# Reading a comparison's node numbers from PSUM, and a GpSimd wait for landed rows at every block's end

## The chip, the core and the metric

The kernel runs on one core of a Trainium2 chip. The metric is the device time of one execution in microseconds (us). Three runs of the kernel before took 4235.66, 4248.94 and 4250.05 us; the median is 4248.94 us. Beside them stands one execution that the hardware profiler recorded, and all durations below are read from it.

The engines are named as the profile names them: PE is TensorE (PEld its weight loads), DVE is VectorE, ACT is ScalarE, POOL is GpSimd, SP is SyncE. A "q" behind a name (POOLq) is the engine's sequencer, which handles waits and branches and hands instructions to the engine.

## The reference

Two layers of a relational graph convolution over 12,500 nodes with 128 channels and 200,000 edges, then a residual and a layer norm. An edge has a type (the argmax over 10 columns of its attributes), a source and a target. For each target node and each type the source rows are averaged, each mean is multiplied by that type's weight matrix, and the ten products are added to a root term and a bias.

```
edge_type = argmax(msg[:, 16:-16], axis=1)            # 10 types
def _rgcn_layer(x, src, dst, edge_type, w_rel, root, bias):
    seg = dst * NUM_REL + edge_type
    sums = segment_sum(x[src], seg, N * NUM_REL)
    cnt = segment_sum(ones, seg, N * NUM_REL)
    mean = (sums / maximum(cnt, 1)[:, None]).reshape(N, NUM_REL, -1)
    return einsum('nrd,rdo->no', mean, w_rel) + x @ root + bias
h = relu(_rgcn_layer(x, ...w_rel1, root1, b1))
out = layernorm(x + _rgcn_layer(h, ...w_rel2, root2, b2))
```

The edges come sorted by target. The kernel has a fast path that relies on this, and a general path behind a flag; with these inputs the fast path runs.

## The kernel before

**Tiling.** The edges are cut into 1563 tiles of 128. Eight tiles are an oct (the last oct has three), two octs belong to a block of 128 target nodes, so a layer has 196 octs and 98 blocks. Seven blocks (PER) are a lap, and 14 laps are a layer. The first and the last lap are written out, the laps between them are a hardware loop on every engine (`laps`, L1259). The two layers run one after the other: layer 2 gathers from the rows that layer 1 wrote.

**POOL (L1288).** For each tile one indirect DMA (`gather`, L1304, its call in the profile as L1305) fetches 128 rows of 512 bytes from memory into `rows[slot, j]`, with the 128 row numbers read from an SBUF tile: `idx_t` for the first 56 gathers, `idx_s` for all others. There are seven slots of eight tiles; oct o uses slot o modulo 7. Every landed gather adds 16 to `rows_in[slot]`. Before an oct, POOL waits for `idx_ready` (L1327), by which ACT says that it has put the oct's numbers into `idx_s`. ACT does this (L1466) as soon as PE has finished the oct that had the slot seven octs earlier. POOL waits for nothing else inside a layer; before layer 2 it waits for `h_saved` (L1323).

**DVE.** For each oct it makes S (`make_S`, L1815): for 8 tiles x 140 columns the comparison of the column numbers 0 to 139 (`iota_c`) with a number per edge (`comb_t`: 10 x the node's place in a window of 14, plus the type). In layer 1 it also makes `hit` and `hit_typ` (L1809, L1811), with which PE counts the edges. Then it adds what PE left in PSUM to a ring of partial sums in SBUF (L1863, and in layer 1 L1836 for the counts), finds the types of edges three blocks ahead (L1781 to L1794), and sums ten products for the block three back (L1899).

**PE.** In `aggregate` (L1585) it waits for S and for the oct's rows (L1588), then multiplies rows by S into one of four PSUM banks. In `transform` (L1611) it multiplies the ring's finished block by the weights. In layer 1 it also turns the types of a block two ahead into `ps_misc` (`turn_types`, L1560), a PSUM bank of 512 columns of which the types take the first 16; DVE copies them out in `take_types` (L1802, L1803).

**Who sets the order.** Each engine's program is written out by hand and runs in order; semaphores tie them. `rows_there` (L1271) gives the count that `rows_in[slot]` has when an oct has landed; before the change only PE uses it.

Of the kernel before, what the change touches and what calls it, by code (L numbers as in the profile page):

```python
# [19 lines left out]
GT = 8  # L20
# [1057 lines left out]
PER = 7  # L1078
# [6 lines left out]
TCOL = TWIN * R  # L1085
# [18 lines left out]
def gnn_kernel(nc, x, src, dst, edge_attr, w_rel1, root1, b1, w_rel2, root2, b2, out, table1, table2,  # L1104
# [5 lines left out]
    with ctx:  # L1110
# [3 lines left out]
        def ps(name):  # L1114
            return ctx.enter_context(nc.psum_tensor(name, [P, 512], F32))
# [19 lines left out]
        held = sem("held")  # L1135
# [14 lines left out]
        S_ready = sem("S_ready")  # L1150
# [101 lines left out]
        ps_agg = [ps(f"ps_agg{q}") for q in range(4)]  # L1252
        ps_y = [ps(f"ps_y{k}") for k in range(3)]
        ps_misc = ps("ps_misc")
        tp_bank = [*ps_y, ps_misc]

        htab = table2[0:N, :]
# [22 lines left out]
        def bc1(ap, n, w):  # L1280
            return ap.rearrange("p (u w) -> p u w", u=1).to_broadcast([P, n, w])
# [6 lines left out]
        @blk.gpsimd  # L1288
        def _(pool):
            g_ = nc.gpsimd  # L1290
            g_.memset(ident[:], 0.0).then_inc(consts_done, 1)
            pool.wait_ge(consts_done, 1)
            g_.affine_select(out=ident[:], in_=ident[:], compare_op=ALU.not_equal, fill=1.0, base=0,
                             pattern=[[-1, P]], channel_multiplier=1).then_inc(consts_done, 1)
            for tile, step, base, mult in ((iota_c, 1, 0, 0), (rev_r, -1, R, 0), (p16, -16, 0, 1), (step_row, P, 0, 0)):
                g_.iota(tile[:], pattern=[[step, tile.shape[1]]], base=base, channel_multiplier=mult,
                        allow_small_or_imprecise_dtypes=True).then_inc(consts_done, 1)
            g_.iota(lap_row[:].rearrange("a (l q) -> a l q", l=LAPS), pattern=[[RN, LAPS], [0, 4 * PER]], base=0,
                    channel_multiplier=0, allow_small_or_imprecise_dtypes=True).then_inc(consts_done, 1)
            g_.memset(eps[:], EPS).then_inc(consts_done, 1)  # L1300
            g_.memset(zero_b[:], 0.0).then_inc(consts_done, 1)
            g_.memset(hit_typ[:], 0.0).then_inc(consts_done, 1)

            def gather(l, slot, j, at):  # L1304
                pool.indirect_dma_start(  # L1305
                    out=rows[:, slot, j, :], out_offset=None, in_=(x, htab)[l][:, :],
                    in_offset=bass.IndirectOffsetOnAxis(ap=at, axis=0)).then_inc(rows_in[slot], 16)


            pool.wait_ge(idx_done, 1)  # L1310
            for o in range(PER):
                for j in range(GT):
                    gather(0, o, j, idx_t[:, o * GT + j:o * GT + j + 1])

            pool.wait_ge(flags_done, 1)
            fast = pool.value_load(flag_i[0:1, 0:1], min_val=0, max_val=1)
            with pool.If(fast < 1):
                pool.wait_ge(clean, 1)
                general_pool(pool)
            with pool.If(fast > 0):  # L1320
                for l in range(2):
                    if l:
                        pool.wait_ge(h_saved, 16 * NBLOCK)  # L1323
                    for i, first, last in laps(pool):
                        for o in range(PER if first and l == 0 else 0, 2 * PER):

                            pool.wait_ge(idx_ready, i * (2 * PER) + (l * OCTS + o + 1 - PER))  # L1327
                            if not isinstance(i, int):
                                pool.sem_inc(held, 1)  # L1329
                            for j in range(tiles_of(o, last)):  # L1330
                                gather(l, o % PER, j, idx_s[:, o % PER, j:j + 1])

        @blk.sync
        def _(sp):
# [202 lines left out]
        def _(pe):  # L1537
# [21 lines left out]
            with pe.If(fast > 0):  # L1559
                def turn_types(s):  # L1560

                    pe.wait_ge(typ_ready, s + 1)
                    for h in range(2):
                        ins = t_.matmul(ps_misc[:, h * GT:(h + 1) * GT], lhsT=typ_a[:, h, :], rhs=pick[:, :],
                                        start=True, stop=True)
                    ins.then_inc(typ_turned, 1)
# [62 lines left out]
                for l in range(2):  # L1629
                    if l == 0:  # L1630
                        turn_types(0)
                        pe.wait_ge(typ_taken, 1)
                        turn_types(1)
                    else:
                        pe.wait_ge(rc_done, NBLOCK)
                        pe.wait_ge(y_taken, NBLOCK * 3 + 3)
                    turn_x(0, l * (LAPS * 16) + 16).then_inc(xt_ready, 1)
                    pe.wait_ge(weights_in[l], 32)
                    for i, first, last in laps(pe):
                        for k in range(PER):  # L1640
                            s = i * PER + k
                            behind = not (first and k < 2)
                            if l == 0 and not (last and k >= PER - 2):
                                pe.wait_ge(typ_taken, s + 2)
                                turn_types(s + 2)
                            if k == 2 and not first:
                                pe.wait_ge(fold_done, i + l * (LAPS - 1))
                            off = offsets(i * (2 * PER) + 2 * k)
                            aggregate(l, i, 2 * k, off, last, ((k - 2) % PER, s * 4 - 2) if behind else None)
                            if behind:  # L1650
                                transform(l, s - 2, (k - 2) % PER, s * 4 - 2,
                                          (i if k > 0 else i - 1) * 16 + (l * LAPS * 16 + 16))
                            off = offsets(i * (2 * PER) + 2 * k + 1)
                            aggregate(l, i, 2 * k + 1, off, last)
                    for b in (NBLOCK - 2, NBLOCK - 1):
                        if l == 0:
                            pe.wait_ge(agg_taken, QUADS + 4)
                            if b == NBLOCK - 1:
                                pe.wait_ge(rc_done, b)
                            turn_counts(ps_misc, 300, b % PER).then_inc(rc_turned, 1)  # L1660
                        transform(l, b, b % PER, QUADS, (l + 1) * LAPS * 16 if b < NBLOCK - 1 else None)

        @blk.vector
        def _(dve):
# [91 lines left out]
            for c in range(1, 4):  # L1756
# [3 lines left out]
            link(v_.tensor_scalar(spread[:, :, :], bc(iota_c[:, 0:16], 16, GT), pm[:, 0:1], -1.0, ALU.is_equal,  # L1760
                                  ALU.mult))

            fast = dve.value_load(flag_i[0:1, 0:1], min_val=0, max_val=1)
            with dve.If(fast < 1):

# [5 lines left out]
            with dve.If(fast > 0):  # L1771
# [41 lines left out]
                                     ).then_inc(hit_ready, 1)  # L1813

                def make_S(g, sl):  # L1815
                    v_.tensor_tensor(S[:, sl, :, :], bc1(iota_c[:, :], GT, TCOL),  # L1816
                                     bc(comb_t[:, bass.ds(g * GT, GT)], GT, TCOL), ALU.is_equal).then_inc(S_ready, 1)

                def places(g):
# [185 lines left out]
```

## Time and profile before

| what | value |
|---|---|
| median of three runs | 4248.94 us |
| profiled execution, own time | 4252.87 us |
| its span | 4251.2 us |
| POOL busy | 3229.2 us, 76% of the span |
| DVE busy | 2271.6 us, 53% |
| PE busy | 2114.3 us, 50% |
| ACT busy | 961.9 us, 23% |
| 16 DMA engines, share of the gathers' queue | 18.4% |
| gathers | 3126 (1507 + 56 in layer 1, 1563 in layer 2) |

A row of the page's fifth part groups the instructions of one line: busy time, the mean of one in ns, and the idle time of the engine just before them with what ended it. "issue" stands for idle time in which the engine waited for nothing that the profile shows. The chain of waits is followed back from the last instruction of the span, or of a window, to whatever released each step. In the chain, a piece "DMA rows<-..." runs from the start of a gather's instruction on POOL to the moment at which its rows have landed.

### The profile page before, as it was taken

Reading aid. Unit: us, or ns where it says so; the run is one execution under the profiler, and the core shown is the slowest. Engines: PE = TensorE matmul, PEld = TensorE weight load, DVE = VectorE, ACT = ScalarE, POOL = GpSimd, SP = SyncE. Lnnn points to the kernel's source line nnn. Section 1 sums busy time; section 2 is a strip of 40 time slices with the busy share of each in tenths; the row PEclk is TensorE's granted clock in tenths of the full one; section 3 lists DMA queues with packets and bytes.
Section 4 is the critical chain, followed back from the end, with each engine's and each line's share of the span. In section 5 each row is a group of like instructions: output and inputs, shape, how many; then the busy total and the mean of one; then the engine's idle time right before and its main releaser. Section 6 shows DMA issues by size and latency. Waiting matters only on the chain.

```text
span 4251.2 us, 55995 instructions
## 1 busy us (share of the span) xinstructions
PE 2114.3 (50%) x12375; PEld 1993.4 (47%) x12376; DVE 2271.6 (53%) x5257; ACT 961.9 (23%) x3133; POOL 3229.2 (76%) x3140
## 2 busy tenths in 40 slices
PE   2544555445444555555545554445545555555554
PEld 2544444444444444444434444444444444444444
DVE  7766666666666666666634444444444444444444
ACT  1222222222222222222212222222222222222222
POOL 7777777777777777777757777777777777777775
PEclk6777777777777777777777777777777677777777
DMA  5222222222222222222212222222222222222221
GB/s 112 72 71 70 71 71 71 68 71 70 71 71 71 72 72 71 71 71 64 53 46 59 62 59 59 59 59 60 59 58 59 60 59 59 59 59 62 57 60 45
DMA packets 206602, 275.41 MB, mean 65 GB/s; under 512 B 62732, under 2 KB 156428, under 8 KB 206444
## 3 DMA queue, kind: packets, MB, share of 16 engines
q0 software_dynamic: 100032, 205.07, 18.4%
q1 hardware_dynamic: 101534, 67.96, 5.7%
q10 hardware_dynamic: 4878, 0.86, 0.2%
q14 instruction: 130, 1.06, 0.1%
q8 instruction: 28, 0.46, 0.0%
HBM read 260.85 MB, written 12.80 MB: 64 GB/s over the span
## 4 chain that ended last, share of the span: by engine, by line
POOL 66%; issue 22%; PE 6%; DVE 3%; DMA 2%; ACT 0%; POOLq 0%; DVEq 0%; ACTq 0%; SPq 0%
POOL rows L1305 66%; PE ps_agg L1603 4%; DVE z_s L1899 1%; PE ps_agg L1599 1%; DMA rows<-in_x_dram,idx_s 1%; DMA rows<-table,idx_s 1%; DVE S L1816 1%; PE ps_y L1622 1%; ACT prod L1504 0%; DVE ring L1863 0%; DVE cnt_ring L1836 0%; POOLq L1327 0%; PE ps_agg L1580 0%; POOLq L1329 0%; ACT idx_s L1466 0%
## 5 line engine op out<-in xcount | busy, mean ns | idle before, releaser
L1305 POOL DMA_INDIRECT rows<-table,idx_s x1563 | 1577.3, 1009 | 506.5 <-issue 472.6
L1305 POOL DMA_INDIRECT rows<-in_x_dram,idx_s x1507 | 1583.5, 1051 | 459.5 <-issue 454.4
L1603 PE MATMUL ps_agg<-S,rows 128*128 128x140 f32 x6272 | 1356.0, 384 | 0.0
L1603 PEld LDWEIGHTS ps_agg<-S,rows 128*128 128x128 f32 x6272 | 1319.2, 283 | 36.4 <-issue 0.2
L1863 DVE TENSOR_TENSOR ring<-ps_agg,ring 128x440 f32 x784 | 483.7, 617 | 1174.2 <-PE ps_agg L1603 1162.8
L1599 PE MATMUL ps_agg<-zero_b 128*128 128x440 bf16 x784 | 379.5, 484 | 1016.9 <-DMA rows<-table,idx_s 818.6
L1836 DVE TENSOR_TENSOR cnt_ring<-ps_agg,cnt_ring 10x14 f32 x1568 | 264.3, 169 | 665.9 <-PE ps_agg L1603 587.2
L1599 PEld LDWEIGHTS ps_agg<-zero_b 128*128 128x128 bf16 x784 | 110.9, 141 | 1070.1 <-issue 1044.5
L1580 PE MATMUL ps_agg<-hit,hit_typ 128*128 128x56 bf16 x392 | 83.9, 214 | 1011.5 <-DMA rows<-in_x_dram,idx_s 878.3
L1899 DVE TENSOR_REDUCE z_s<-prod 128x128 f32<-128x1536 f32 (+1 forms) x196 | 563.8, 2876 | 6.0 <-ACT prod L1509 5.5
L1466 ACT COPY idx_s<-idx_t 128x8 uint32 (+1 forms) x385 | 75.9, 197 | 2165.3 <-PE ps_agg L1603 2165.3
L1580 PEld LDWEIGHTS ps_agg<-hit,hit_typ 128*128 128x128 bf16 x392 | 45.4, 116 | 1032.9 <-issue 1032.9
L1504 ACT ACTIVATE prod<-ps_y,rc_s 128x128 f32<-128x128 f32 x1960 | 527.7, 391 | 6.2
L1622 PE MATMUL ps_y<-wall,ring 128*128 128x128 f32 x3920 | 520.1, 285 | 6.5 <-ACT prod L1504 5.0
L1816 DVE TENSOR_TENSOR S<-iota_c,comb_t 128x1120 f32<-128x1120 f32 x392 | 517.9, 1321 | 4.2 <-issue 2.2
L1622 PEld LDWEIGHTS ps_y<-wall,ring 128*128 128x128 f32 x3920 | 508.6, 205 | 6.9 <-issue 5.3
L1511 ACT COPY ring<-zero_f 128x1280 f32<-128x1280 f32 x196 | 265.2, 1353 | 0.0
L1489 ACT ACTIVATE h_s<-z_s 128x128 f32<-128x128 f32 x98 | 30.4, 310 | 620.2 <-DVE z_s L1899 620.2
L1493 ACT ACTIVATE std<-mv,eps 128x1 f32<-128x1 f32 x98 | 28.8, 294 | 434.8 <-DVE mv L1906 426.7
L1305 POOL DMA_INDIRECT rows<-in_x_dram,idx_t x56 | 64.6, 1154 | 23.9 <-issue 16.8
L1625 PE MATMUL ps_y<-root,xt_s 128*128 128x128 f32 x392 | 76.0, 276 | 0.0
L1509 ACT COPY prod<-ps_y 128x128 f32<-128x128 f32 x196 | 69.3, 354 | 0.0
(114 smaller groups left out, 969.5 us busy)
## 6 DMA issues: line engine op xcount, KB each, us to landing
attr<-in_edge_attr_dram SPq DMA_DIRECT2D x97, 336.0 KB, 3.0
rows<-table,idx_s POOLq DMA_INDIRECT x1563
rows<-in_x_dram,idx_s POOLq DMA_INDIRECT x1507
x_in<-in_x_dram SPq DMA_DIRECT2D x97, 64.0 KB, 1.9
table<-h_s SPq DMA_DIRECT2D x97, 64.0 KB
x_in<-table SPq DMA_DIRECT2D x97, 64.0 KB, 1.9
prod<-in_x_dram SPq DMA_DIRECT2D x97, 64.0 KB
out_dram<-o_s SPq DMA_DIRECT2D x97, 64.0 KB
```

The source lines that it names most:

```text
L1305: pool.indirect_dma_start(out=rows[:, slot, j, :], out_offset=None, in_=(x, htab)[l][:, :], in_offset=bass.IndirectOffsetOnAxis(ap=at, axi ...
L1504: ins = a_.activation(prod[:, 2 + r, :], ps_y[q][:, c * C:(c + 1) * C], ACT.Copy, scale=rc_s[:, r:r + 1])
L1511: a_.copy(ring[:, :, at * P:(at + 1) * P], zero_f[:, 0:1].rearrange("p (a u) -> p a u", a=1) .to_broadcast([P, R, P])).then_inc(ring_zeroe ...
L1580: t_.matmul(bank[:, CCOL:RCOL], lhsT=hit_typ[:, sl, 4 * h:4 * h + 4, :].rearrange("p c r -> p (c r)"), rhs=hit[:, sl, 4 * h:4 * h + 4, :]. ...
L1599: t_.matmul(bank[:, 0:QCOL], lhsT=zero_b[:, 0:P], rhs=zero_b[:, 0:QCOL], start=True, stop=False)
L1603: ins = t_.matmul(bank[:, bass.ds(off[j] * R, TCOL)], lhsT=rows[:, o % PER, j, :], rhs=S[:, o % PER, j, :], start=False, stop=(c == 3))
L1622: ins = t_.matmul(ps_y[q][:, c * C:(c + 1) * C], lhsT=ring[:, r, k * P:(k + 1) * P], rhs=wall[l][:, r, :], start=True, stop=True)
L1625: ins = t_.matmul(ps_y[q][:, 2 * C:3 * C], lhsT=xt_s[:, :], rhs=root[l][:, :], start=True, stop=True)
L1816: v_.tensor_tensor(S[:, sl, :, :], bc1(iota_c[:, :], GT, TCOL), bc(comb_t[:, bass.ds(g * GT, GT)], GT, TCOL), ALU.is_equal).then_inc(S_rea ...
L1836: ins = v_.tensor_tensor(win, bank[32 * c:32 * c + R, at:at + TWIN], win, ALU.add)
L1863: v_.tensor_tensor(win, bank[:, 0:QCOL].rearrange("p (n r) -> p r n", r=R), win, ALU.add).then_inc(agg_taken, 1)
L1899: v_.tensor_reduce(out=z_s[:, :], in_=prod[:, lo:hi, :].rearrange("p r o -> p o r"), op=ALU.add, axis=AX.X).then_inc(red_done, 1)
```

## The change

Three things change. Line numbers of the changed kernel differ by up to nine from those of the one before.

- A view `iota_p` of 140 columns (320 to 459) of the PSUM bank `ps_misc` gets a copy of `iota_c` once, before the fast path starts. `make_S` reads it in place of `iota_c`. Its other input, `comb_t`, stays in SBUF.
- PE, before it turns the types of the next block but one into the same bank, waits in addition until S of the octs up to the end of the block before has been made.
- POOL, after the gathers of each block's second oct, waits until all eight gathers of that oct have landed. The last block of each layer has no such wait, and the first 56 gathers are issued ahead of this code. Inside the loop of laps it also adds 1 to `held`, a semaphore on which nobody waits.

```
+        iota_p = ps_misc[:, 320:320 + TCOL]
...
                             for j in range(tiles_of(o, last)):
                                 gather(l, o % PER, j, idx_s[:, o % PER, j:j + 1])
+                            if o % 2 == 1 and not (last and o == 2 * PER - 1):
+
+                                pool.wait_ge(rows_in[o % PER], rows_there(l, i, o, last))
+                                if not isinstance(i, int):
+                                    pool.sem_inc(held, 1)
...
                             if l == 0 and not (last and k >= PER - 2):
                                 pe.wait_ge(typ_taken, s + 2)
+                                pe.wait_ge(S_ready, s * 2 + 2)
                                 turn_types(s + 2)
...
+            link(v_.tensor_copy(iota_p, iota_c[:, :]))
...
                 def make_S(g, sl):
-                    v_.tensor_tensor(S[:, sl, :, :], bc1(iota_c[:, :], GT, TCOL),
+                    v_.tensor_tensor(S[:, sl, :, :], bc1(iota_p, GT, TCOL),
                                      bc(comb_t[:, bass.ds(g * GT, GT)], GT, TCOL), ALU.is_equal).then_inc(S_ready, 1)
```

POOL's program at the head of the loop over laps 1 to 12 of layer 1, before: each oct is one gather that waits for its numbers and seven more.

```order
L1265 ISA
L1305 DMA rows<-in_x_dram,idx_s 128x128 [waits idx_ready]
L1305 DMA rows<-in_x_dram,idx_s 128x128 x7
L1327 REGISTER_ALU
L1305 DMA rows<-in_x_dram,idx_s 128x128 [waits idx_ready]
L1305 DMA rows<-in_x_dram,idx_s 128x128 x7
L1327 REGISTER_ALU
L1305 DMA rows<-in_x_dram,idx_s 128x128 [waits idx_ready]
```

The same place after the change:

```order
L1266 ISA
L1306 DMA rows<-in_x_dram,idx_s 128x128 [waits idx_ready]
L1306 DMA rows<-in_x_dram,idx_s 128x128 x7
L1328 REGISTER_ALU
L1306 DMA rows<-in_x_dram,idx_s 128x128 [waits idx_ready]
L1306 DMA rows<-in_x_dram,idx_s 128x128 x7
L1335 ISA
L1328 REGISTER_ALU [waits rows_in1]
L1306 DMA rows<-in_x_dram,idx_s 128x128 [waits idx_ready]
```

After 16 gathers the sequencer computes the count and waits for `rows_in1`, before the step that works out the next `idx_ready` count. No gather changes its place.

PE's program at the start of a block of that loop in layer 1, after the change (MATMUL into ps_misc turns the types, MATMUL into ps_agg counts the block's first oct):

```order
L1651 ISA [waits typ_taken]
L1568 REGISTER_ALU [waits S_ready]
L1570 MATMUL ps_misc<-pick,typ_a 128x8 [waits typ_ready]
L1570 MATMUL ps_misc<-pick,typ_a 128x8
L1575 ISA
L1575 TENSOR_LOAD off_i
L1593 REGISTER_ALU
L1594 ISA [waits S_ready]
L1597 ISA [waits rows_in0]
L1586 MATMUL ps_agg<-hit,hit_typ 128x56 [waits hit_ready,agg_taken]
```

The wait on `S_ready` ahead of the two type matmuls is the added one; the one at L1594 stood there before.

## Rows read from the trace of the kernel before

**Rows 1.** The page: span; engines: busy us (share) xinstructions; the chain that ended last.

```profile
span 4251.2 us, 55995 instructions
PE 2114.3 (50%) x12375; PEld 1993.4 (47%) x12376; DVE 2271.6 (53%) x5257; ACT 961.9 (23%) x3133; POOL 3229.2 (76%) x3140
...
POOL 66%; issue 22%; PE 6%; DVE 3%; DMA 2%; ACT 0%; POOLq 0%; DVEq 0%; ACTq 0%; SPq 0%
```

**Rows 2.** The waits: engine line <- releaser: us in total, times, longest us.

```profile
POOL rows L1305 <- issue: 943.8, 3095, 0.3
PE ps_agg L1580 <- DMA rows<-in_x_dram,idx_s: 878.3, 165, 9.8
POOL rows L1305 <- ACT idx_s L1466: 8.8, 29, 0.3
```

**Rows 3.** The page's groups: busy us, mean ns of one | idle before.

```profile
L1305 POOL DMA_INDIRECT rows<-table,idx_s x1563 | 1577.3, 1009 | 506.5 <-issue 472.6
L1305 POOL DMA_INDIRECT rows<-in_x_dram,idx_s x1507 | 1583.5, 1051 | 459.5 <-issue 454.4
...
L1305 POOL DMA_INDIRECT rows<-in_x_dram,idx_t x56 | 64.6, 1154 | 23.9 <-issue 16.8
```

**Rows 4.** Line 1305's instructions: duration ns min/median/max, first and last start us.

```profile
L1305 POOL DMA_INDIRECT rows<-table,idx_s x1563: 943/947/2097, 2166.5 to 4219.2; - x196
```

**Rows 5.** Timeline, layer 1: start us, us, engine line op out<-in xcount.

```profile
1305.41 1.31 DVE L1816 TENSOR_TENSOR S<-iota_c,comb_t 128x1120 f32<-128x1120 f32 x1
1305.67 1.87 POOL L1305 DMA_INDIRECT rows<-in_x_dram,idx_s  x1 [0.30 <-issue]
...
1309.05 0.62 DVE L1863 TENSOR_TENSOR ring<-ps_agg,ring 128x440 f32 x1
1309.09 0.95 POOL L1305 DMA_INDIRECT rows<-in_x_dram,idx_s  x1 [0.30 <-issue]
```

**Rows 6.** The chain of waits in windows: start us, us, what.

```profile
1344.63 2.69 DMA rows<-in_x_dram,idx_s
...
1366.51 2.50 DMA rows<-in_x_dram,idx_s
...
3404.33 2.61 DMA rows<-table,idx_s
...
3500.07 2.53 DMA rows<-table,idx_s
```

**Rows 7.** The chain around layer 2's first gather, which waited for a landing.

```profile
2164.78 1.49 DMA table<-h_s
2166.27 0.26 issue
```

**Rows 8.** The chain at an oct's boundary inside the loop.

```profile
1318.49 0.03 POOLq L1327
...
1318.78 0.94 POOL rows L1305
```

**Rows 9.** DVE's sums with PSUM and without: duration ns min/median/max.

```profile
L1863 DVE TENSOR_TENSOR ring<-ps_agg,ring x784: 601/617/620, 76.2 to 4228.5; 128x440 f32 x196
...
L1871 DVE TENSOR_TENSOR ring<-ring x26: 605/609/614, 199.9 to 4108.0; 128x440 f32<-128x440 f32 x26
```

**Rows 10.** Timeline of one block in layer 1, PE and DVE.

```profile
1325.19 0.19 PE L1580 MATMUL ps_agg<-hit,hit_typ 128*128 128x56 bf16 x1 [1.46 <-DMA rows<-in_x_dram,idx_s]
...
1327.28 1.32 DVE L1816 TENSOR_TENSOR S<-iota_c,comb_t 128x1120 f32<-128x1120 f32 x1
...
1327.54 0.19 PE L1564 MATMUL ps_misc<-pick,typ_a 128*128 128x8 bf16 x2
...
1331.69 0.17 DVE L1802 COPY typ_t<-ps_misc 128x16 f32 x1
...
1337.47 0.21 PE L1580 MATMUL ps_agg<-hit,hit_typ 128*128 128x56 bf16 x1 [9.74 <-DMA rows<-in_x_dram,idx_s]
```

More of the change, by code:

```diff
@@ L1254, in gnn_kernel @@
         ps_misc = ps("ps_misc")
+        iota_p = ps_misc[:, 320:320 + TCOL]
         tp_bank = [*ps_y, ps_misc]
@@ L1331, in _ @@
                                 gather(l, o % PER, j, idx_s[:, o % PER, j:j + 1])
+                            if o % 2 == 1 and not (last and o == 2 * PER - 1):
+                                pool.wait_ge(rows_in[o % PER], rows_there(l, i, o, last))
+                                if not isinstance(i, int):
+                                    pool.sem_inc(held, 1)
         @blk.sync
@@ L1644, in _ @@
                                 pe.wait_ge(typ_taken, s + 2)
+                                pe.wait_ge(S_ready, s * 2 + 2)
                                 turn_types(s + 2)
@@ L1761, in _ @@
                                   ALU.mult))
+            link(v_.tensor_copy(iota_p, iota_c[:, :]))
             fast = dve.value_load(flag_i[0:1, 0:1], min_val=0, max_val=1)
@@ L1815, in make_S @@
                 def make_S(g, sl):
-                    v_.tensor_tensor(S[:, sl, :, :], bc1(iota_c[:, :], GT, TCOL),
+                    v_.tensor_tensor(S[:, sl, :, :], bc1(iota_p, GT, TCOL),
                                      bc(comb_t[:, bass.ds(g * GT, GT)], GT, TCOL), ALU.is_equal).then_inc(S_ready, 1)
```

## The prediction, made before the changed kernel ran

> **What bounds the kernel now.** I read the page's shares and its chain first. POOL is busy for 76% of the span, more than any other engine, and the chain that ended last runs 66% over POOL and 22% over "issue" [rows 1]. The waits say whose "issue" that is: POOL stood idle 3095 times for 943.8 us with nothing to wait for, 0.30 us a time, and in all 8.8 us for the numbers that ACT hands over, while PE sat waiting for gathered rows for hundreds of us [rows 2]. So the gathers set the pace: each costs its instruction plus 0.30 us, 3126 in a row, and PE, DVE and ACT follow behind. Whatever makes a gather longer, or opens a gap between two gathers, goes one to one into the time; what DVE or PE do costs nothing as long as they keep up.
>
> Next come the gathers themselves. Their means are 1051 ns and 1009 ns [rows 3], but the median is 947 ns with a maximum of 2097 [rows 4]. A few gathers are long, the rest are all alike. The timeline shows which: the gather that starts at 1305.67, just after DVE began S, takes 1.87 us and ends 0.82 us after S does. A gather that starts in the middle of DVE's sum out of PSUM (L1863) takes the plain 0.95 us [rows 5]. The difference between the two DVE instructions is that S takes both inputs from SBUF and the sum takes one of them from PSUM. The gather reads its row numbers from SBUF soon after its start, and seems to be held there until S is done.
>
> The Trainium skill has a rule for this ("SBUF — State Buffer", section Who interferes with whom): a DVE instruction with two SBUF inputs contends with a GpSimd instruction that reads SBUF, one with at most one SBUF input does not. The same section also speaks against the change: its probe did not see `tensor_tensor` stall a DMA, and it infers that descriptor generation needs the write side, which `tensor_tensor` leaves alone. By the first rule the edit to S gives back all the excess, by the second nothing. The trace takes the first one's side, for these gathers at least (1.87 against 0.95 us).
>
> **Term 1, S read from PSUM: minus 258 us.** The excess over 947 ns is 1507 x 0.104 = 156.7 us in layer 1 and 1563 x 0.062 = 96.9 us in layer 2 [rows 3, 4]. The first 56 gathers have 56 x 0.207 = 11.6 us more, most of it from DVE's start-up work, which stays; I give S 4 us of it. Together 258 us. Bounds: nothing, if the one input left in SBUF (`comb_t`) still holds the gather, and 265 us, all of it. The nearest row is the sum at 1309.05, with the same pairing of one PSUM and one SBUF input, and a gather passes it unhurt [rows 5]: I take 258. S itself hardly changes: a sum of 440 columns takes 617 ns with a PSUM input and 609 without [rows 9], and DVE has room (53% busy).
>
> **Term 2, what is left of the two-input work: plus 7 us.** `hit` and `hit_typ` in layer 1 (98 blocks, two pairs each) also read SBUF twice, for about 0.43 us together. So far S came right behind and took the blame for both. One pair will now fall just after the block-end wait, between two reads as I place it; the other may meet a gather. A gather comes every 1.25 us, so the chance is 0.43 / 1.25 = 0.34 and the loss then about 0.2 us: 98 x 0.07 = 7 us. Bounds: 0, and 196 x 0.4 = 78 us if every pair meets a gather, which can happen since the whole cycle is locked to the gathers.
>
> **Term 3, the block-end wait: plus 316 us.** The waits are counted from the loops: in layer 1 four in lap 0 (octs 7, 9, 11, 13), 84 in laps 1 to 12 and 6 in the last, in layer 2 7 + 84 + 6, so 94 + 97 = 191. At each, POOL's sequencer stands until the eighth gather's rows have landed, and everything queued behind it, the next block's 16 gathers, starts late. Nothing on POOL can fill the gap. From the start of a gather to its landing the chain shows 2.69, 2.50, 2.61 and 2.53 us, mean 2.58, of which 0.95 is the instruction: the rows land 1.63 us after it ends [rows 6]. Then the restart: after the wait for layer 1's rows POOL's first gather began 0.26 us after the landing [rows 7]. In the loop the step through L1327 and L1329 to the gather takes 1318.78 - 1318.49 = 0.29 us [rows 8], and the new wait stands before it, so I take 0.32. The 0.30 us between any two gathers is saved. Net 1.63 + 0.32 - 0.30 = 1.65 us, times 191 = 316 us (rounded up from 315). Bounds: landing 1.55 and restart 0.26 give 1.51 and 288 us; landing 1.74 and restart 0.45, for the branch at a lap's end, give 1.89 and 361 us. Who waits for it: PE, for the next block's rows, 1.65 us longer per block. It has nothing else to do in that time.
>
> A second sentence of the skill bears on this term. "DMA: Bandwidth & Descriptors", section Anatomy of one DMA, puts a GpSimd DMA at about 2.0 us plus its bytes over 436 GB/s, 2.15 us for 64 KB. If that held from the gather's start, the landing would come 1.20 us after its end and the term would be 233 us. The four rows say 2.50 to 2.69, so the trace disagrees; it is a rival below.
>
> **Term 4, PE's added wait: nothing.** In a block of layer 1 PE begins the second oct at 1325.19, DVE makes the S that is now waited for from 1327.28 to 1328.60, and PE turned the types at 1327.54. They will be turned about 1.1 us later, at 1328.7. DVE fetches them at 1331.69, and PE's next oct starts only at 1337.47, when rows land [rows 10]. So the delay is covered twice, by 3 us of DVE's other work and by 8.8 us of PE's idle time. The cover would be gone only if DVE fell behind POOL, and even then POOL feels it only after seven octs of lead. The one copy into PSUM at the start is some 0.3 us on DVE while POOL is still at its first 56 gathers: nothing.
>
> **Sum.** 4252.87 - 258 + 7 + 316 = 4318 us against the profiled execution. That execution ran 3.9 us over the median of the three runs, so against the median the figure is 4314 us, 1.5% slower than 4248.94. The two large terms nearly cancel, and the point of balance is easy to state: the waits cost more than S gives back as soon as one costs over 258 / 191 = 1.35 us.
>
> **Rivals.**
> - *S still holds the gathers* (the one SBUF input is enough, or the stall comes from something else that runs beside S). Then only the waits are left: 4314 + 258 = 4572 us. For it: I see the stall, not the port. Against it: the sum at 1309.05. Chance 0.05.
> - *Other two-input work takes over the stalls.* If both pairs hit a gather in every block, term 2 is up to 78 us: about 4385 us. For it: everything is phase-locked, so a meeting in one block is a meeting in all. Against it: the pairs are a third as long as S. Chance 0.07.
> - *The landing is short when no gather follows* (the other side). If the rows landed 1.20 us after the instruction's end once POOL falls silent, a wait would cost 1.20 + 0.32 - 0.30 = 1.22 us, 233 us in all, and the time would be 4314 - 83 = 4231 us, 0.4% below before. It decides from 1.35 us per wait downwards, that is from a landing under 1.33 us. For it: all my rows have another gather coming behind. Against it: the four rows lie within 0.2 us of each other, in both layers, and the lowest is 0.2 us above that point. Chance 0.08.
> - *The wait does not bite.* POOL's sequencer runs ahead of its engine, and if the count awaited were already there when it came to the wait, only term 1 would be left: about 3998 us. The count is the one that PE uses for the same oct, and PE does wait for it, so this is nearly excluded. Chance 0.02.
>
> **How the numbers follow.** My forecast, both large terms at about full size, has 0.78; by its own bounds it runs from 4252.87 - 265 + 288 - 4 = 4272 to some 4370 us (waits at 361, others at 20). A measurement of this kernel can tell about 0.5%, 21 us, from no change, so "same" is 4228 to 4270. The forecast's low end stops just above it, and I leave 0.03 of its chance there. The landing rival splits evenly between same and faster. So faster 0.02 + 0.04 = 0.06; same 0.03 + 0.04 = 0.07; slower 0.75 + 0.05 + 0.07 = 0.87. Range 4266 to 4370 us.
>
> **What will show it.** The gathers' mean falls to about 950 ns in both layers and the long ones beside S are gone (term 1; if the mean stays over 1000 the first rival holds). In layer 1 a few gathers of 1.1 to 1.3 us stand beside `hit` (term 2). POOL shows a new wait for landed rows, 191 times for 1.9 to 2.0 us each, 372 us in total (term 3). PE's types come 1 us later with no new wait on DVE (term 4). POOL's busy time falls to about 2970 us while the span grows. I am wrong if a wait costs under 1.4 us, or if POOL's idle time moves to waits for ACT or for anything but DMAs.

## The result, and the profile after

The changed kernel takes 4432.49 us (median of three runs, 4432.33 to 4433.56) against 4248.94: a ratio of 1.0443, 95% interval 1.0411 to 1.0474. The prediction was 4314 us, 4266 to 4370. The direction was right. The time lies 118 us above the forecast and 62 above the top of the range.

The page of the changed kernel, in the order of [rows 1, 3]:

```profile
span 4430.8 us, 56330 instructions
...
PE 2096.7 (47%) x12375; PEld 1966.7 (44%) x12376; DVE 2270.4 (51%) x5258; ACT 960.1 (22%) x3133; POOL 2963.1 (67%) x3140
...
POOL 54%; issue 26%; DMA 10%; PE 7%; DVE 2%; ACT 1%; POOLq 0%; DVEq 0%; ACTq 0%; SPq 0%
...
L1306 POOL DMA_INDIRECT rows<-table,idx_s x1563 | 1475.0, 944 | 731.3 <-issue 480.8
L1306 POOL DMA_INDIRECT rows<-in_x_dram,idx_s x1507 | 1424.5, 945 | 681.0 <-issue 470.9
```

The gathers' means fell from 1009 (layer 2) and 1051 ns (layer 1) to 944 and 945. POOL works 266 us less (3229.2 to 2963.1) while the span grows by 179.6 us. The chain now holds 10% of DMA: POOL stands until rows land. The waits of the changed kernel, to be read beside [rows 2], and what the view of the gathers' line says of who waited for a gather:

```profile
POOL rows L1306 <- issue: 968.5, 2921, 3.0
POOL rows L1306 <- DMA rows<-table,idx_s: 212.6, 86, 2.8
POOL rows L1306 <- DMA rows<-in_x_dram,idx_s: 207.7, 83, 3.4
```

```profile
  PE ps_agg L1605: 1003.1, 165
  PE ps_agg L1586: 962.9, 174
  POOL rows L1306: 484.9, 191
```

The last line has all 191 waits: 484.9 us idle, or 2.54 us each. The usual gap of 0.305 us would have stood at each anyway, so they cost 484.9 - 58.3 = 426.6 us. Outside them, 20 gaps between two gathers are 1.32 us long instead of 0.305, another 20.3 us. The sum closes: -266.1 + 426.6 + 20.3 = +180.8 us, against 179.6 measured in the span.

One wait, as the chain of waits has it (start us, us, what), in the loop of laps in layer 1:

```profile
1308.24 2.55 DMA rows<-in_x_dram,idx_s
1310.80 0.03 issue
1310.82 0.02 POOLq L1337
1310.84 0.06 issue
1310.90 0.03 POOLq L1328
1310.94 0.04 issue
1310.98 0.02 POOLq L1330
1311.00 0.75 issue
1311.75 0.94 POOL rows L1306
```

The rows land at 1310.80, 2.55 us after the gather's start. That is what the forecast took from [rows 6]. But the next gather starts only at 1311.75. The counter instruction behind the wait (L1337), the arithmetic for the next count (L1328) and the second counter (L1330) take 0.2 us with the pauses between them, and 0.75 us more pass before the engine starts. What fills the 0.75 us no view shows. The forecast had 0.32 us for all of this.

S and the gathers beside it, and PE's types, in the timeline of the next microseconds:

```profile
1313.38 1.31 DVE L1825 TENSOR_TENSOR S<-ps_misc,comb_t 128x1120 f32<-128x1120 f32 x1
...
1314.25 0.94 POOL L1306 DMA_INDIRECT rows<-in_x_dram,idx_s  x1 [0.30 <-issue]
...
1314.82 0.20 PE L1570 MATMUL ps_misc<-pick,typ_a 128*128 128x8 bf16 x2 [1.17 <-DVE S L1825]
...
1317.90 0.23 DVE L1820 TENSOR_TENSOR hit_typ<-iota_c,typ_t 128x80 bf16<-128x80 f32 x1
1317.99 0.96 POOL L1306 DMA_INDIRECT rows<-in_x_dram,idx_s  x1 [0.30 <-issue]
1318.05 1.31 DVE L1825 TENSOR_TENSOR S<-ps_misc,comb_t 128x1120 f32<-128x1120 f32 x1
...
1323.45 0.20 PE L1586 MATMUL ps_agg<-hit,hit_typ 128*128 128x56 bf16 x1 [8.43 <-DMA rows<-in_x_dram,idx_s]
```

A gather that begins during S, or 0.06 us before it, now takes 0.94 to 0.96 us where [rows 5] had 1.87. PE turns the types 1.17 us late, and long after that still waits 8.43 us for rows.

### The profile page after: what moved, and what is told of

Read it like the earlier page. It is cut to its first block, busy times and chain, and to the rows that moved or that the text cites. A ratio compares the mean times of both kernels' runs of the same rounds, so it can differ in the third digit from the quotient of the medians.

```text
span 4430.8 us, 56330 instructions
## 1 busy us (share of the span) xinstructions
PE 2096.7 (47%) x12375; PEld 1966.7 (44%) x12376; DVE 2270.4 (51%) x5258; ACT 960.1 (22%) x3133; POOL 2963.1 (67%) x3140
## 3 DMA queue, kind: packets, MB, share of 16 engines
q14 instruction: 130, 1.06, 0.1%
## 4 chain that ended last, share of the span: by engine, by line
POOL 54%; issue 26%; DMA 10%; PE 7%; DVE 2%; ACT 1%; POOLq 0%; DVEq 0%; ACTq 0%; SPq 0%
POOL rows L1306 54%; DMA rows<-in_x_dram,idx_s 5%; DMA rows<-table,idx_s 5%; PE ps_agg L1609 5%; PE ps_agg L1605 1%; DVE z_s L1908 1%; DVE S L1825 1%; PE ps_y L1628 1%; ACT prod L1510 0%; ACT idx_s L1472 0%; DVE ring L1872 0%; DVEq L1829 0%; POOLq L1330 0%; DMA nat_s<-in_src_dram 0%; POOLq L1328 0%
## 5 line engine op out<-in xcount | busy, mean ns | idle before, releaser
L1306 POOL DMA_INDIRECT rows<-table,idx_s x1563 | 1475.0, 944 | 731.3 <-issue 480.8
L1306 POOL DMA_INDIRECT rows<-in_x_dram,idx_s x1507 | 1424.5, 945 | 681.0 <-issue 470.9
L1609 PE MATMUL ps_agg<-S,rows 128*128 128x140 f32 x6272 | 1324.3, 377 | 0.0
L1609 PEld LDWEIGHTS ps_agg<-S,rows 128*128 128x128 f32 x6272 | 1284.5, 276 | 34.9 <-issue 0.4
L1628 PEld LDWEIGHTS ps_y<-wall,ring 128*128 128x128 f32 x3920 | 518.6, 208 | 8.4 <-issue 6.6
L1825 DVE TENSOR_TENSOR S<-ps_misc,comb_t 128x1120 f32<-128x1120 f32 x392 | 516.3, 1317 | 4.2 <-issue 2.2
L1570 PE MATMUL ps_misc<-pick,typ_a 128*128 128x8 bf16 x196 | 20.4, 175 | 112.3 <-DVE S L1825 55.6
```

The lines of the kernel that those rows point to most:

```text
L1306: pool.indirect_dma_start(out=rows[:, slot, j, :], out_offset=None, in_=(x, htab)[l][:, :], in_offset=bass.IndirectOffsetOnAxis(ap=at, axi ...
L1609: ins = t_.matmul(bank[:, bass.ds(off[j] * R, TCOL)], lhsT=rows[:, o % PER, j, :], rhs=S[:, o % PER, j, :], start=False, stop=(c == 3))
L1628: ins = t_.matmul(ps_y[q][:, c * C:(c + 1) * C], lhsT=ring[:, r, k * P:(k + 1) * P], rhs=wall[l][:, r, :], start=True, stop=True)
L1825: v_.tensor_tensor(S[:, sl, :, :], bc1(iota_p, GT, TCOL), bc(comb_t[:, bass.ds(g * GT, GT)], GT, TCOL), ALU.is_equal).then_inc(S_ready, 1)
```

## The experiments

The theory after the result: each wait costs the landing (1.63 us after the gather's end) plus a restart that depends on what stands between the landing and the next gather, 0.3 us if the gather carries its wait and 0.95 us or more if instructions of the sequencer's own stand there; S from PSUM takes the stalls away by itself; PE's wait costs nothing. Rivals: the slow restart belongs to the landing or to the loop whatever stands there; or a wait and a counter cost 0.6 us each time even without standing.

The runs came in six sets, each with runs of the kernel before beside it. In five of them the kernel before took 4768 to 4847 us, and GpSimd was then not the bound: it waited for numbers that ACT handed over late. I call these the late sets. One set, e9 to e12, had the kernel before at 4242.97 us, as in the comparison above. Each ratio is against the kernel before in the same set. Only the ratios of e9 to e12 bear on the result. From the late sets I read single durations in the trace, and the end of this part tells what differs there. Their traces also lack some semaphore records (e3 and e4 hold 286 updates of ACT's number semaphore, the changed kernel's trace 385).

**S alone from PSUM (e1, e5, e9).** The changed kernel without the block-end wait:

```
-                            if o % 2 == 1 and not (last and o == 2 * PER - 1):
-                                pool.wait_ge(rows_in[o % PER], rows_there(l, i, o, last))
-                                if not isinstance(i, int):
-                                    pool.sem_inc(held, 1)
```

> The change without POOL's wait: S read from PSUM and PE's added wait alone. Theory A (the gathers' instructions lose 266 us, and the wait at the block's end costs everything else): the profiled execution before, 4253 us, less 266 is 3987 us, ratio 0.938; gathers at 943 to 947 ns on average and no gap over 0.31 us between two gathers. Rival B (part of the gain comes from the wait, which moves the gathers away from DVE's work): the mean gather stays over 960 ns and the time over 4030 us.

> The kernel of e1 again, since before took 4834 us beside e1 and 4249 us at first, and e1's trace shows PE, not POOL, as the one that is waited for. Where before takes about 4249 us: theory A says 3987 us, ratio 0.938, gathers at 943 to 947 ns and no gap over 0.31 us; rival B says a mean gather over 960 ns and over 4030 us; rival F (with POOL faster, PE or DVE bounds the kernel at once) says 4100 us or more with POOL waiting for ACT's numbers. Where before takes about 4830 us again: ratio 1.00, as e1.

> S reads the node numbers from PSUM, and GpSimd waits for no landing. Theory D (the gathers' loss is the waits' alone): the 3070 gathers take 943 to 946 ns, as in the changed kernel. On a chip where the kernel before takes about 4249 us, where GpSimd's gathers are the bound, the time is the changed kernel's less its 427 us of waiting and 20 us of added gaps, 3985 us (3960 to 4020), ratio 0.938. Rival W (the landings of the gathers limit the octs anyway): there the time falls by less than 100 us, and GpSimd's gathers wait for ACT's idx or their own queue. Where the kernel before takes 4770 us or more, both expect a ratio of 1.003 to 1.004, as twice measured, and the run tells nothing new.

e1: 4848.16 against 4834.28 us, 1.0035 [1.0025, 1.0045]. e5: 4790.79 against 4774.12, 1.0037 [1.0018, 1.0055]. In both GpSimd wasn't the bound, and the expected gain in time did not come. The gathers' mean was 943 to 946 ns all the same, as expected, so rival B on the mean is out. e9, where GpSimd is the bound: 3990.38 against 4242.97 us, 0.9402 [0.938, 0.9423]. Page and timeline of e9:

```profile
span 3984.1 us, 56081 instructions
...
POOL 69%; issue 24%; PE 4%; DVE 1%; DMA 1%; ACT 0%; POOLq 0%; DVEq 0%; SPq 0%; ACTq 0%
...
L1306 POOL DMA_INDIRECT rows<-table,idx_s x1563 | 1475.2, 944 | 506.0 <-issue 475.8
L1306 POOL DMA_INDIRECT rows<-in_x_dram,idx_s x1507 | 1423.6, 945 | 459.3 <-issue 452.3
```

```profile
1202.71 0.26 DVE L1813 TENSOR_TENSOR hit<-iota_c,rel_t 128x112 bf16<-128x112 f32 x1
1202.89 0.23 DVE L1815 TENSOR_TENSOR hit_typ<-iota_c,typ_t 128x80 bf16<-128x80 f32 x1
...
1203.04 1.31 DVE L1820 TENSOR_TENSOR S<-ps_misc,comb_t 128x1120 f32<-128x1120 f32 x1
1203.29 0.94 POOL L1306 DMA_INDIRECT rows<-in_x_dram,idx_s  x1 [0.30 <-issue]
```

The span is 267.1 us shorter than that of the kernel before in the first comparison, and the gathers' busy time 265.8 us. The medians of the set itself differ by 252.6 us, 245 to 263 by the interval. So what the gathers lose in length the time loses too, one to one within that scatter, and the added PE wait, which is in this kernel, costs nothing that shows. Between two gathers of the loop no gap is over 0.32 us. This version beats both kernels. It came out inside the range expected (3960 to 4020 us), and the rivals with PE, DVE or the landings as the next bound (4100 us or more, or under 100 us gained) are out.

**The changed kernel again (e10).** The same text, beside e9, e11 and e12.

> The changed kernel as it is, beside the kernels of this call. Where the kernel before takes about 4249 us: ratio 1.044, the 191 waits each 0.94 to 0.95 us from the landing to the next gather in the loop. Where the kernel before takes 4770 us or more, GpSimd's gathers are not the bound: by theory D the wait costs there only what is not covered by idle time that GpSimd has anyway; the sum of s_only (+17 us) and wait alone (-36 us) gives -19 us, ratio 0.996 (0.985 to 1.010). Rival (the wait's cost is paid at any chip): +184 us, ratio 1.038.

4438.47 against 4242.97 us, 1.0456 [1.0433, 1.048]. It is the base for e11 and e12: 191 waits with 484.4 us of idle time, and 20 gaps.

**GpSimd's laps written out (e3, e6, e11).** With known lap numbers no counter instruction is issued and the count awaited is a constant:

```
-                    for i, first, last in laps(pool):
+                    for i, first, last in [(n, n == 0, n == LAPS - 1) for n in range(LAPS)]:
```

> The changed kernel with POOL's 14 laps written out, so that every wait has a constant and is carried by the gather behind it. In the changed kernel's trace the next gather began 0.26 to 0.33 us after the landing in the written-out laps, 0.95 in the loop and 1.27 at its end. Theory D (the restart depends on how the wait is handed over; 0.30 everywhere): less 144 x 0.64 + 24 x 0.96 = 115 us, about 4317 us; with the 20 extra gaps of 1.0 us gone too, 4297. Rival E (the restart grows with the stretch of work, not with the form of the code): 4432 us, no change from the changed kernel.

> The kernel of e3 again, for the same reason. Where before takes about 4249 us: theory D (the restart depends on how the wait is handed over) says a restart of about 0.30 us at all 191 waits and 4297 to 4317 us, ratio 1.01 to 1.016; rival E (the restart does not depend on the form of the code) says 4432 us, ratio 1.043. Where before takes about 4830 us: ratio 1.01, as e3.

> The changed kernel with GpSimd's laps written out one after the other, so that a gather carries its own wait and no separate instruction stands between the landing and it. Theory D: from the landing to the next gather 0.3 us instead of 0.95 (1.27 at a lap's end) wherever the idx is there in time; on a chip where the kernel before takes about 4249 us the time is 4432 - 115 (restarts) = 4317 us, and 4297 us if the 20 added gaps of 1.0 us go as well. Rival E (the restart is the landing's own delay, not the loop's): 0.95 us stays and the time is 4432. Where the kernel before takes 4770 us or more, both expect only a ratio of 1.011 to 1.016, as twice measured.

e3: 4884.34, 1.0109 [1.009, 1.0129]. e6: 4842.82, 1.0158 [1.0126, 1.019]; in neither was GpSimd the bound, so the times say nothing of the restart. e11: 4296.07 us, 1.0122 [1.0099, 1.0145] against the kernel before and 142.4 us less than e10. Its chain at a block's end:

```profile
1308.73 2.50 DMA rows<-in_x_dram,idx_s
1311.24 0.26 issue
1311.50 0.95 POOL rows L1306
```

The landing is the same, the restart is 0.26 us, at all 191 waits (0.257 to 0.259). The idle time at the waits is 361.2 us, 123.2 less than in e10, and the 20 gaps are gone (20.3 us): 143.5 us, against 142.4 measured. The forecast with both effects was 4297 us. Rival E, a restart that belongs to the landing, is out.

**Written out, but with the counter instructions (e4).** As e3, and `sem_inc(held, 1)` issued in every lap, before each oct and behind each wait.

> As e3, but after each wait the sequencer adds 1 to the unused semaphore, as the loop does, so the wait is an instruction of its own ahead of the gather. Theory D1 (0.95 us is the price of a gather whose wait stands in an instruction of its own): restart 0.85 to 0.95 us at all 191 waits, about 4317 + 120 = 4430 us. Theory D2 (the price comes from the loop's registers and branch): restart 0.30 to 0.40, about 4320 us.

4908.36 against 4834.28 us, 1.015 [1.0131, 1.0169], a late set again, so the time decides nothing. In its trace a landing was the last thing waited for at only 31 of the 191 waits. GpSimd stood at least 2.35 us at each of them, in the median 2.46, and the restart reads 0.89 to 1.29 us (once 1.48), never 0.3. In e3 there are 39 such waits, in the median 1.86 us long; 19 restarts are 0.26 us and the others read 0.33 to 0.86. Where a landing's record is missing, a restart reads too long, so the idle times are the safer comparison: 0.6 us more in e4. So the loop itself isn't needed for the slow restart; a wait and counters in instructions of their own are enough. Which of them does it isn't separated.

**A wait after every oct (e12).**

```
-                            if o % 2 == 1 and not (last and o == 2 * PER - 1):
+                            if not (last and o == 2 * PER - 1):
```

> The changed kernel with the wait after every oct instead of every second: about 382 waits instead of 191. Theory D: each is 1.6 us to the landing and 0.95 us of restart in the loop; on a chip where the kernel before takes about 4249 us the time grows by 191 x 2.23 = 426 us to 4858 us (4800 to 4900), less whatever of the 20 gaps of 1.0 us the waits hide. The gaps: if they are tied to time (one each 202 us, hidden wherever the sequencer is ahead), they stay as far apart in us and there are about 22; if they are tied to the count of octs (one each 18), they stay 18 octs apart and about 222 us. Rival F (the second wait finds its rows landed, since the transfers run on during the first): under 1.0 us for each added wait, time under 4630. Where the kernel before takes 4770 us or more, the waits' lengths tell the same, and the total time does not.

4860.55 us, 1.145 [1.1424, 1.1476], 422.1 us over e10. The 192 added waits cost 412 us over the usual gap, 2.15 us each, the old ones 419.7 instead of 426.1, and there are 38 gaps for 20, 18.3 us more: 424 in all. So the price is linear, the time is the one expected (4858 us), and rival F of this run (the second wait finds its rows landed) is out. The gaps came out by neither of my two cases. Inside the loops they stand 9 octs (72 gathers, 111 us) apart in e12, and 18 octs (144 gathers, 202 us) in the changed kernel. Here is one of each, in the changed kernel and in e12:

```profile
369.95 0.94 POOL rows L1306
370.90 1.32 issue
372.22 0.94 POOL rows L1306
```

```profile
283.08 0.94 POOL rows L1306
284.02 1.32 issue
285.34 0.95 POOL rows L1306
```

They fit a hitch of the sequencer every 72 gathers, seen only where it has just stood and has no lead: in the changed kernel every second one falls in the middle of a block and is covered. The traces of the late sets agree: in e7 they appear at octs 14, 32, 41, 50 also in the kernel before, behind waits for late numbers. But standing alone isn't enough. In e11 GpSimd stood 1.8 to 2.0 us ahead of the same octs (14, 32, 50 and on), started again within 0.26 us, and no gap followed. So the gap goes with the slow restart or with a longer stand. What the hitch is, and why the quick restart hides it, stays open.

**The wait alone (e8, e13, e16).** As the changed kernel, with S reading `iota_c` again:

```
-                    v_.tensor_tensor(S[:, sl, :, :], bc1(iota_p, GT, TCOL),
+                    v_.tensor_tensor(S[:, sl, :, :], bc1(iota_c[:, :], GT, TCOL),
```

> The changed kernel with S read from SBUF again, so POOL's wait alone beside PE's. Where before takes about 4249 us: if the two parts simply add, 4249 + 427 + 20 = 4696 us, ratio 1.105; the rival is that the stalls beside S fall partly into POOL's idle time at the block's end and count once: 4600 to 4650 us. Where before takes about 4800 us: 4850 to 4950 us, since POOL is not the bound there and the wait is paid only in part.

> Only the block-end wait and its counter instruction are added; S still reads its numbers from SBUF. Theory D: the wait's 427 us and the 20 gaps of 1.0 us come whole, and the gathers keep the stalls from S, except that some of DVE's S operations now fall into the 191 idle stretches of 2.5 us and stall nothing: the mean gather is between 0.945 and 1.05 us. With all of the 266 us of stalls left: 4249 + 447 = 4696 us, ratio 1.105; if a third of them falls into the waits: 4607 us, 1.084. Range 4600 to 4700. Rival I (the waits and the stalls hide one another, so the wait costs much less where the gathers are slow): under 4550 us. Where the kernel before takes 4770 us or more, the run repeats e8 (ratio 0.9925).

> As for e13, for a chip where the kernel before takes about 4249 us: by theory D 4696 us (ratio 1.105) with all of the stalls left, 4607 us (1.084) if a third of DVE's S operations falls into the idle stretches; by rival I (waits and stalls hide one another) under 4550 us. Where the kernel before takes 4770 us or more, it repeats 0.99.

e8: 4735.73 against 4767.95 us, where 4850 to 4950 was expected, 0.9925 [0.9896, 0.9953]. e13: 4803.72 against 4846.96, 0.9893 [0.9855, 0.9931]. e16: 4797.74 against 4834.22, 0.9921 [0.9892, 0.9949]. All three fell where GpSimd isn't the bound, so the price of the wait with slow gathers beside it was never timed; the 1.105 or 1.084 expected stay untested. The gathers kept their stalls (means 1002 to 1008 ns, in the kernel before of e7 1010 and 1006), so it is the edit to S, not the wait, that removes them. Why the wait makes the kernel slightly faster there is open.

**A wait for rows that have long landed (e2, e14, e15).**

```
-                                pool.wait_ge(rows_in[o % PER], rows_there(l, i, o, last))
+                                pool.wait_ge(rows_in[(o - 1) % PER], rows_there(l, i, o - 1, last))
```

> The changed kernel, but POOL waits at each block's end for the rows of the block's first oct, which have long landed by then. Same number and form of waits and semaphore increments. Theory A (the price is the drain: landing 1.62 us, then a restart with an empty queue): no wait bites, so as e1, about 3990 us. Rival C (the added semaphore instructions themselves cost, since the restart took 0.95 us inside the loop): 191 x 0.6 us more than e1, about 4100 us.

> The changed kernel, but each of the 191 waits is for the rows of the oct before the block's last one, which landed some 7 us earlier. Theory D (the cost is the sequencer's standing until the landing, and then fetching the next instructions): GpSimd never stands, its sequencer stays gathers ahead, and neither the 0.95 us of restart nor the gaps of 1.0 us are seen: the time is that of S alone, ratio 0.940 (3990 us, 3980 to 4010). Rival G (a wait and a counter instruction in the loop cost 0.6 us each time by themselves): 191 x 0.63 = +120 us, 4110 us, ratio 0.968. Where the kernel before takes 4770 us or more, both expect 1.005.

> As for e14, for a chip where the kernel before takes about 4249 us: by theory D (GpSimd's sequencer never stands, since the rows waited for landed some 7 us earlier) 3990 us, ratio 0.940, no idle stretch over 0.31 us between two gathers of the loop; by rival G (a wait and a counter instruction in the loop cost 0.6 us each time by themselves) 4110 us, ratio 0.968. Where the kernel before takes 4770 us or more, both expect 1.005.

e2: 4854.56 against 4834.28 us, 1.0051 [1.0032, 1.007]. e14: 4865.81, 1.0049 [1.0029, 1.007]. e15: 4858.89 against 4834.22, 1.0048 [1.0032, 1.0065]. The times don't tell, the traces do in part. Of the block ends in the loop at which, as far as the records tell, ACT's numbers were there in time, 55 of 79, 63 of 82 and 52 of 70 show no gap over 0.31 us, as this one of e15 (the last gather of oct 25 and the first of oct 26, with the wait between them):

```profile
319.32 0.94 POOL L1306 DMA_INDIRECT rows<-in_x_dram,idx_s  x1 [0.30 <-issue]
320.57 0.95 POOL L1306 DMA_INDIRECT rows<-in_x_dram,idx_s  x1 [0.31 <-issue]
```

In the changed kernel none of the 168 waits in the loop does. A wait and its counter instruction thus cost the engine nothing where the sequencer is ahead, which speaks against rival G. The remaining 18 to 24 have gaps of mostly 0.6 to 1.6 us; there the sequencer had little lead, and I can't tell a cost of the instructions from that. A time where GpSimd is the bound is missing.

**The kernel before, once more (e7).**

> The kernel before, unchanged, for a trace of its own: it took 4249 us at first and 4834 and 4774 us beside the later runs. If this chip gives about 4249 us, the trace repeats the one above and serves as the base of the other runs on this chip. If it gives about 4800 us, the theory is that the gathers are as before (947 ns median, stalls beside S of some 260 us), while PE and DVE have gaps of issue of 1 us and more between their instructions, and POOL waits for ACT's numbers because PE is late. The rival is that the gathers themselves land later or take longer there.

One execution, 4761.72 us beside 4767.95: the kernel before on its own is as slow, so the 12% lie in the set, not in an edit. Its chain, two of its waits, and for contrast PE's group in e7 and in e9:

```profile
another core or an unknown queue 28%; issue 26%; DVE 21%; DVEq 10%; PE 10%; ACT 2%; POOL 1%; DMA 0%; ACTq 0%; SPq 0%; POOLq 0%
```

```profile
PE ps_agg L1603 <- issue: 672.7, 706, 3.1
POOL rows L1305 <- ACT idx_s L1466: 570.3, 157, 10.0
```

```profile
L1603 PE MATMUL ps_agg<-S,rows 128*128 128x140 f32 x6272 | 1330.5, 349 | 681.9 <-issue 672.7
```

```profile
L1604 PE MATMUL ps_agg<-S,rows 128*128 128x140 f32 x6272 | 1326.6, 377 | 0.0
```

GpSimd is 1% of the chain here, where it was 66% in [rows 1]. PE stands idle 673 us between the matmuls of one group, waiting for nothing that the profile shows, and GpSimd waits 570 us for ACT's numbers where [rows 2] had 8.8. ACT hands them over when PE has finished an oct, so a late PE fits this; but DVE has a larger share of the chain than PE, and 28% of it is followed to nothing, so which engine is the bound isn't shown. GpSimd's shorter gathers went into longer waits for ACT: 815 us in e1 and 781 us in e5, where e7 has 570. That fits their gaining nothing there. The granted TensorE clock was 0.677 in e7 and 0.745 in e9, but the matmuls of this group were not busy longer for it (1330.5 against 1326.6 us). The cause is open. It isn't the chip alone, since one chip gave 4774 us in e5's set and 4243 in e9's.

## Why the prediction was wrong, by its own steps

**What bounds the kernel: right.** Both large effects came one to one, and e9 and e12 show it in times. All of this holds for the sets in which the kernel before takes about 4249 us.

**Term 1, -258 us: right.** The gathers' busy time fell by 266 us. The excess over the median was 265 us before and is 8.5 us after, of which 2 are term 2's. So the stalls beside S gave back 259 us, as forecast. The other 9 us come from the plain gather, 944 ns in the median here and 947 before (3 ns x 3126). That isn't owed to S: in e2, e14 and e15, where S also comes from PSUM, the median is 947 again. That the sum of the two meets the upper bound of 265 is luck. In e9 the median time moved by 253 us. The rival "S still holds the gathers" is out. The rule of the Trainium skill, "SBUF — State Buffer", section Who interferes with whom, on two SBUF inputs holds here (1.87 us beside S from SBUF, 0.94 to 0.96 with one input in PSUM); its remark that a probe did not see `tensor_tensor` stall a DMA does not hold for these gathers.

**Term 2, +7 us: mis-sized, about 2 us.** Layer 1's 1507 gathers are busy 1424.5 us, 1.9 us over the median of 944 ns for each. The longest of them takes 1.06 us, so the forecast's sign, a few of 1.1 to 1.3 us, did not come. In e9's timeline the pair at 1202.71 lies between the starts of two gathers and is over when the one at 1203.29 begins; in the changed kernel `hit_typ` at 1317.90 reaches 0.14 us into a gather, which takes 0.96 us for it instead of 0.94. The rival on this is out.

**Term 3, +316 us: this is the step that failed, and within it the restart.** The 191 waits were counted right. The landing was right: 1.63 us after the gather's end, mean of all 191, forecast 1.63; so "the landing is short" is out too. The restart was put at 0.32 us. It measures 0.91 us in the mean. In the 23 written-out waits it is 0.26, but for the two at which the loop is entered (0.95 and 0.96). At the 144 inside the loop it is 0.95 in the mean (0.89 to 0.96). At the 24 at a lap's end it is 1.27 in the mean: 1.29 to 1.36 where another lap follows, 0.93 at the two where the loop is left. The extra 0.59 us x 191 = 113 us are the miss. The sign of being right, waits of 1.9 to 2.0 us and 372 us in total, failed with it (2.54 us, 484.9 us). I had two rows for it and read both wrongly. The first [rows 7] is a gather that carries its own wait, with no instruction between: true of the written-out laps and of e11, not of the loop. The second [rows 8] I took for a restart. But the sequencer runs about four gathers ahead: at all 300 passes through L1327 the next gather to start is the oct's fifth, and the oct whose numbers L1327 counts begins four gathers later. So the gather at 1318.78 was already handed over. That 0.29 us was part of the usual gap. The change puts a counter instruction and the arithmetic of L1328 between wait and gather; I gave them no price because in [rows 8] they seemed to have none.

**Missing term, +20 us.** The same lead had been covering a hitch of 1.0 us. Each wait takes the lead away, and behind slow restarts 20 hitches come to light. The rival "the wait does not bite" is out: all 191 did.

**Term 4, nothing: right.** PE's types come 1.17 us later, and PE still waits 8.43 us for rows. In e9, which has this wait, nothing of it shows between the gathers.

Together: the waits cost 427 us instead of 316 (111 more; the restart's 113, less what was rounded), the gaps 20, and from this go 1 in term 1, 5 in term 2 and the plain gather's 9, which no step forecast. That is 116 us over the forecast. The spans differ by 179.6 us where -258 + 7 + 316 = 65 was forecast, 115 more. Against the medians it is 118, because the profiled execution before ran 3.9 us over its median. The range failed for the same reason: its upper end of 361 us let the restart grow to 0.45 us only, from 0.26 us, although no row showed GpSimd start again in the loop after standing empty. The honest upper bound was "never seen here". The point of balance at 1.35 us per wait was right: the measured 2.23 us is far beyond it. Even the 0.26 us restart of e11, with the gaps gone, gives 1.59 us per wait, and e11 is still slower than the kernel before.

## What to carry to other kernels

An engine's sequencer that runs ahead, here by about four gathers, hides its own instructions; a wait that empties this lead costs the wait plus everything that was hidden. Price the restart from a place where the engine really stood empty before the same instructions, and if no row has one, say so and leave the range open upwards. When a change bundles a gain and a cost, split them: S from PSUM alone is 6% faster, the bundle 4% slower.

## What the runs showed of the hardware that I had not expected

- From a landing to GpSimd's next gather: 0.26 us if the gather carries its wait (all 191 waits of e11), 0.95 us with a counter instruction, one arithmetic step and another counter between (144 waits of the changed kernel), 1.27 us in the mean at the end of a hardware loop's pass (24 waits). The instructions themselves take 0.2 us of the 0.95.
- Gaps of 1.0 us over the usual stand 72 gathers apart in e12's loops. They show only where GpSimd has just stood, and not behind the restarts of 0.26 us in e11.
- The same program took 4243 to 4249 us in some sets and 4768 to 4847 in others. In the late sets PE stood idle between matmuls of one group with no cause shown, and GpSimd was no longer the bound: the ratio of one and the same edit was 0.940 in the first and 1.004 in the others.
